# A state-space and expert block on one core: the state's output by 64-row matmuls in pairs

## The reference

```python
xz = layernorm(x) @ w_in;  xp, z = split(xz, 2)            # 512 channels each
xc = silu(causal_conv4(xp) + conv_b)
def step(h, xt):
    h = h * 0.9 + 0.1 * (xt @ w_B)                         # w_B: 512 x 16
    return (h, h @ w_C)                                    # w_C: 16 x 512
_, ys = scan(step, 0, xc)
x = x + (ys * silu(z)) @ w_out
...
h = gelu(x_norm @ W1[e] + b1[e]);  x = x + sum over 2 experts of (h @ W2[e] + b2[e]) / 2
```

## Time and profile before

| | us |
|---|---|
| median of 3 runs | 508.88 (508.84 to 509.13) |
| the profiled execution, its own time | 509.31 |
| its span, first to last instruction | 507.5 |
| PE busy | 503.0 (99%) |
| DVE busy | 452.3 (89%) |
| ACT busy | 400.7 (79%) |
| POOL busy | 348.2 (69%) |
| granted TensorE clock | 1.000 of full |

### The profile page before, as it was taken

One profiled execution on the slowest core, in us unless ns is written; L12 is line 12 of the kernel. 1 busy time (PEld: TensorE's weight loads), 2 busy tenths in 40 slices (PEclk: granted clock), 3 DMA queues, 4 the chain that ended last, 5 costly groups with the idle time before them and its releaser, 6 DMA issues.

```text
span 507.5 us, 9839 instructions
## 1 busy us (share of the span) xinstructions
PE 503.0 (99%) x3026; PEld 447.6 (88%) x3026; DVE 452.3 (89%) x896; ACT 400.7 (79%) x692; POOL 348.2 (69%) x390
## 2 busy tenths in 40 slices
PE   8999999999999999999999999999999999999997
PEld 8889799898898989989899998989989899998997
DVE  6999899999998899989999899998999989996773
ACT  4986958878869788697887969779797887969454
POOL 4959597659693796928969197772977649673391
PEclk9999999999999999999999999999999999999999
DMA  8940005344251432606235170432604333130102
GB/s 266 292 174 12 32 0 173 119 131 162 74 182 37 165 124 83 206 17 193 79 124 165 42 223 24 165 124 86 203 40 143 106 125 125 51 115 0 43 3 83
DMA packets 53379, 57.28 MB, mean 113 GB/s; under 512 B 8682, under 2 KB 49642, under 8 KB 53226
## 3 DMA queue, kind: packets, MB, share of 16 engines
q1 hardware_dynamic: 51498, 56.67, 34.1%
q10 hardware_dynamic: 1856, 0.31, 0.3%
HBM read 35.46 MB, written 21.50 MB: 112 GB/s over the span
## 4 chain that ended last, share of the span: by engine, by line
PE 97%; DVE 1%; DMA 1%; issue 0%; DVEq 0%
PE blk L1291 16%; PE blk L1292 16%; PE blk L1296 16%; PE tok L1410 12%; PE tok L1408 12%; PE tok L1409 12%; PE turn L1449 3%; PE turn L1452 3%; PE blk L1471 3%; PE turn L1239 1%; PE tok L1291 1%; PE tok L1296 1%; PE tok L1292 1%; DMA x_mid<-in_L_attn_x 1%; DVE stats_t L914 0%; DVE normed L931 0%
## 5 line engine op out<-in xcount | busy, mean ns | idle before, releaser
L989 DVE SCALAR_TENSOR_TENSOR conv<-blk,tap_w,conv 128x512 f32<-128x512 f32 x192 | 130.1, 740 | 8.2 <-ACT conv L680 7.6
L485 POOL TENSOR_TENSOR y_lo<-gate,y_hi 128x512 fp32r<-128x512 f32 x57 | 72.2, 1299 | 36.6 <-ACT y_hi L608 36.5
L1291 PE MATMUL blk<-xn_hi,w_in_hi 128*128 128x512 f32 x228 | 89.5, 393 | 0.0
L1292 PE MATMUL blk<-xn_hi,w_in_lo 128*128 128x512 f32 x228 | 89.1, 391 | 0.0
L450 POOL TENSOR_TENSOR xc_lo<-conv,xc_hi 128x512 fp32r<-128x512 f32 x60 | 72.7, 1229 | 8.3 <-ACT xc_hi L608 8.1
L1408 PE MATMUL tok<-w_out_hi,y_hi 128*128 128x256 f32 x256 | 72.1, 282 | 0.0
L1410 PE MATMUL tok<-w_out_hi,y_lo 128*128 128x256 f32 x256 | 71.9, 281 | 0.0
L1409 PE MATMUL tok<-w_out_lo,y_hi 128*128 128x256 f32 x256 | 71.9, 281 | 0.0
L1296 PE MATMUL blk<-xn_lo,w_in_hi 128*128 128x512 f32 x228 | 70.3, 389 | 0.0
L1408 PE MATMUL tok<-w_hi,hid_hi 128*128 128x256 f32 x248 | 69.9, 282 | 0.0
L1410 PE MATMUL tok<-w_hi,hid_lo 128*128 128x256 f32 x248 | 69.7, 281 | 0.0
(11 more groups left out here) (189 smaller groups left out, 1321.7 us busy)
## 6 DMA issues: line engine op xcount, KB each, us to landing
spill<-normed SPq DMA_DIRECT2D x25, 512.0 KB, 2.8
normed<-spill SPq DMA_DIRECT2D x100, 128.0 KB, 2.8
out<-x_mid SPq DMA_DIRECT2D x30, 256.0 KB, 2.7
x_mid<-in_L_attn_x SPq DMA_DIRECT2D x29, 256.0 KB, 2.7
x_in<-in_L_attn_x SPq DMA_DIRECT2D x14, 512.0 KB, 4.3
w_all<-in_L_ffn_W SPq DMA_DIRECT2D x2, 2048.0 KB, 11.8
b_all<-in_L_ffn_b SPq DMA_DIRECT2D x1, 1024.0 KB, 13.1
gate<-in_L_attn_w_in SPq DMA_DIRECT2D x2, 256.0 KB, 4.5
```

The costliest lines, as they stand in the source:

```text
L485: nc.gpsimd.tensor_tensor(y_lo[:, j, :], gate_of(o, j), y_hi[:, j, :].bitcast(F32), ALU.subtract).then_inc(y_lo_set, 1)
L989: nc.vector.scalar_tensor_tensor(cols, blk[j][:], tap_w[:, j, t:t + 1], cols, ALU.mult, ALU.add).then_inc(tap_added, 1)
L1291: mm(dst, whi(k), his(k), start=(k == 0), stop=False)
L1292: mm(dst, wlo(k), his(k), start=False, stop=False)
```

## The change

- **TensorE.** `state_out` multiplies over 64 rows in place of 128. Blocks 0 and 2 use rows 0 to 63 of `c_mix` and `state_mix`, blocks 1 and 3 rows 64 to 127. Still four matmuls of 512 columns, into the same banks, in the same order. In the steps (not in the opening) the wait for a free bank is taken for two blocks at a time, ahead of the first of them, so the second has no wait.
- **Layout.** Each half of 64 rows is the same: four groups of 16, where `b_mix` holds w_B rounded in groups 0, 1, 2 and the rest of w_B in group 3. `state_mix` becomes: rounded state in groups 0, 2, 3 and the rest of the state in group 1. `c_mix`: rounded w_C in groups 0, 1, 3 and the rest in group 2. The products of two rests are left out.
- **Masks.** Four columns of one number per row are made once by VectorE from the identity matrix at the start (`row_masks`): `low_rows` is 1 in the group that holds a rest and 0 elsewhere, `sign_rows` is -1 there and 1 elsewhere.
- **ScalarE** now rounds state times `sign_rows` (a scale read per row, in place of a constant); **VectorE** does state * `low_rows` + `state_mix` over 128 rows in one scalar_tensor_tensor, in place of a subtraction over 64 rows; **GpSimd**, for chunk 1, does it in two instructions, one that multiplies the state by the mask and, after a wait on it, an addition.
- **Constants in the opening.** `b_mix`: three ScalarE instructions of 128 numbers per row in place of four of 64, two GpSimd subtractions in place of four. `c_mix`: a GpSimd multiplication and an addition over 128 rows in place of two subtractions over 32 rows.

```diff
+        def mix_cols(h, group):
+            return slice(h * HALF + group * NST, h * HALF + (group + 1) * NST)
...
             def state_lo(a, q):
                 pool.wait_ge(norm2_ready, TT - EARLY)
                 pool.wait_ge(h_hi, a + 1)
-                nc.gpsimd.tensor_tensor(state_mix[P // 2:P, :], state[P // 2:P, q, :],
-                                        state_mix[P // 2:P, :].bitcast(F32), ALU.subtract).then_inc(h_lo, 1)
+                nc.gpsimd.tensor_scalar(state[:, q, :], state[:, q, :], low_rows[STATE][:], None, ALU.mult).then_inc(h_masked, 1)
+                pool.wait_ge(h_masked, 1)
+                nc.gpsimd.tensor_tensor(state_mix[:], state[:, q, :], state_mix[:].bitcast(F32), ALU.add).then_inc(h_lo, 1)
...
             def state_hi(a, q):
                 act.wait_ge(scanned, a + 1)
-                hi(state_mix[:], state[:, q, :]).then_inc(h_hi, 1)
+                hi(state_mix[:], state[:, q, :], sign_rows[STATE][:]).then_inc(h_hi, 1)
...
             def state_lo(a, q):
                 dve.wait_ge(h_hi, a + 1)
-                lo(state_mix[P // 2:P, :], state[P // 2:P, q, :], state_mix[P // 2:P, :]).then_inc(h_lo, 1)
+                nc.vector.scalar_tensor_tensor(state_mix[:], state[:, q, :], low_rows[STATE][:], state_mix[:].bitcast(F32), ALU.mult,
+                                               ALU.add).then_inc(h_lo, 1)
...
+            def row_masks():
+                dve.wait_ge(consts_set, 3)
+                groups = ident[:].rearrange("p (h g i) -> p g h i", h=2, i=NST)
+                for i, group in enumerate(LOW_GROUP):
+                    nc.vector.tensor_reduce(low_rows[i][:], groups[:, group], axis=mybir.AxisListType.XY,
+                                            op=ALU.add).then_inc(rows_set, 1)
+                for i in range(2):
+                    dve.wait_ge(rows_set, 1 + i)
+                    nc.vector.tensor_scalar(sign_rows[i][:], low_rows[i][:], -2.0, 1.0, ALU.mult, ALU.add).then_inc(rows_set, 1)
+
             def opening():
+                row_masks()
...
             def state_out(a, s, js=range(JD)):
                 pe.wait_ge(h_lo, a + 1)
...
-                    mm(c_bank(a, j)[:], c_mix[:, j * P:(j + 1) * P], state_mix[:], start=True,
+                together = 2 if has_ffn(s) else 1
+                for i, j in enumerate(js):
+                    if i % together == 0:
+                        c_free(a, s, js[i + together - 1])
+                    rows = slice(j % 2 * HALF, (j % 2 + 1) * HALF)
+                    mm(c_bank(a, j)[:], c_mix[rows, j * P:(j + 1) * P], state_mix[rows, :], start=True,
                        stop=True).then_inc(c_ready, 1)
```

More of the change, by code:

```diff
@@ L35, in build_block @@
     HALO = TAPS - 1
-    REP = P // (2 * NST)
-    assert PER == 2 and TT == 4 and KD == 2 and JD == 4 and JF == 4 and NST == 16 and E == 8
+    HALF = P // 2
+    STATE, WEIGHT = 0, 1
+    LOW_GROUP, REST_GROUP = (1, 2), 3
+    assert PER == 2 and TT == 4 and KD == 2 and JD == 4 and JF == 4 and HALF == 4 * NST and E == 8
     x_t = x.rearrange("b s d -> (b s) d").rearrange("(c n p) d -> c p n d", p=P, n=TT)
@@ L66, in build_block @@
         unused = sb("unused", [1, 1])
+        low_rows, sign_rows = [sb(f"low_rows{i}", [P, 1]) for i in range(2)], [sb(f"sign_rows{i}", [P, 1]) for i in range(2)]
         first_tok = sb("first_tok", [P, KD])
@@ L117, in build_block @@
         consts_set = sem("consts_set")
+        rows_set = sem("rows_set")
         w_hi_set = sem("w_hi_set")
@@ L148, in build_block @@
         u_ready, scanned = sem("u_ready"), sem("scanned")
-        h_hi, h_lo = sem("h_hi"), sem("h_lo")
+        h_hi, h_masked, h_lo = sem("h_hi"), sem("h_masked"), sem("h_lo")
         c_ready = sem("c_ready")
@@ L512, in opening @@
                 norm1(1)
-                pool.wait_ge(w_hi_set, 5 + REP)
-                for r in range(REP):
-                    nc.gpsimd.tensor_tensor(b_mix[:, :, (2 * r + 1) * NST:(2 * r + 2) * NST], wb_raw[:],
-                                            b_mix[:, :, 2 * r * NST:(2 * r + 1) * NST].bitcast(F32),
-                                            ALU.subtract).then_inc(mix_lo_set, 1)
-                for i, r in enumerate((P // 4, 3 * P // 4)):
-                    rows = slice(r, r + P // 4)
-                    pool.wait_ge(mix_lo_set, REP + i)
-                    nc.gpsimd.tensor_tensor(c_mix[rows, :], state[rows, 0, :], c_mix[rows, :].bitcast(F32),
-                                            ALU.subtract).then_inc(mix_lo_set, 1)
-                pool.wait_ge(mix_lo_set, REP + 2)
+                pool.wait_ge(w_hi_set, 5 + REST_GROUP)
+                for h in range(2):
+                    nc.gpsimd.tensor_tensor(b_mix[:, :, mix_cols(h, REST_GROUP)], wb_raw[:],
+                                            b_mix[:, :, mix_cols(h, 0)].bitcast(F32), ALU.subtract).then_inc(mix_lo_set, 1)
+                pool.wait_ge(rows_set, 4)
+                nc.gpsimd.tensor_scalar(state[:, 0, :], state[:, 0, :], low_rows[WEIGHT][:], None, ALU.mult).then_inc(mix_lo_set, 1)
+                pool.wait_ge(mix_lo_set, 3)
+                nc.gpsimd.tensor_tensor(c_mix[:], state[:, 0, :], c_mix[:].bitcast(F32), ALU.add).then_inc(mix_lo_set, 1)
+                pool.wait_ge(mix_lo_set, 4)
                 split_conv(0, (0, 1))
@@ L624, in mix_hi @@
                 hi(state[:, 0, :], raw_c, GAIN).then_inc(w_hi_set, 1)
-                for r in range(REP):
-                    hi(b_mix[:, :, 2 * r * NST:(2 * r + 1) * NST], wb_raw[:]).then_inc(w_hi_set, 1)
-                act.wait_ge(w_hi_set, 4 + REP)
-                hi(c_mix[:], state[:, 0, :]).then_inc(w_hi_set, 1)
+                for group in range(REST_GROUP):
+                    both = b_mix[:].rearrange("p j (h c) -> p j h c", h=2)[:, :, :, mix_cols(0, group)]
+                    hi(both, wb_raw[:].rearrange("p j (o s) -> p j o s", o=1).broadcast_to([P, JD, 2, NST])).then_inc(w_hi_set, 1)
+                act.wait_ge(w_hi_set, 4 + REST_GROUP)
+                act.wait_ge(rows_set, 4)
+                hi(c_mix[:], state[:, 0, :], sign_rows[WEIGHT][:]).then_inc(w_hi_set, 1)
             def turn1_hi(c):
@@ L1453, in state_in, with c_free @@
                 ins.then_inc(u_ready, 1)
+            def c_free(a, s, j):
+                if has_ffn(s):
+                    pe.wait_ge(gelu_set, (s - 2) * JF + j + 1)
+                elif a == 0:
+                    pe.wait_ge(gate_set, JD + j + 1)
+                elif j == 0:
+                    pe.wait_ge(route_step, 1)
+                elif j == 1:
+                    pe.wait_ge(tap_added, last_tap(2, 2))
+                elif j == 2:
+                    pe.wait_ge(gate_set, 3 * JD - 1)
+                else:
+                    pe.wait_ge(tap_added, last_tap(2, 3))
             def state_out(a, s, js=range(JD)):
                 pe.wait_ge(h_lo, a + 1)
[L1457 to L1471 removed]
+                together = 2 if has_ffn(s) else 1
[4 more added lines that the diff above has]
+                    mm(c_bank(a, j)[:], c_mix[rows, j * P:(j + 1) * P], state_mix[rows, :], start=True,
                        stop=True).then_inc(c_ready, 1)
```

19 lines of the change are left out of this document (3 added, 16 removed).

## The result

The changed kernel takes 511.9 us (median of 4 runs, 511.66 to 513.09) where the kernel before, run beside it, takes 509.0: a ratio of 1.0061, with a 95% interval of 1.0044 to 1.0079. The prediction said 506.4 and a range of 505.0 to 510.0. It is slower, not faster, and outside the range. The profiled execution took 511.66 with a span of 509.8 (before 509.31 and 507.5), so the traces stand 2.3 us apart.

What follows compares the result with a forecast made beforehand. TensorE, busy 99%, was taken as the bound, if VectorE (89%) keeps up. Boundary gains of 3.28 us less 0.80 lost in the opening gave -2.48: 506.8 profiled, 506.4 in medians; range 505.0 to 510.0.

Steps and rivals of the forecast that it cites:

- I take no price for the change of form: TensorE at state_out: switching matmul form costs nothing, so each state_out takes 0.56 us for 0.93, a gain of 0.37.
- a change of form costs as much as an exposed load on either side: Rival at state_out: 0.10 us lost on either side, gain 0.17 per state_out, 508.0 us in all; chance 0.12.
- I let the second of a pair start 0.10 late: TensorE at state_out: the second matmul's exposed weight load delays it 0.10 us; starts at 0, 0.10, 0.23, 0.33.
- the rival's pairs: Rival at state_out: both loads go ahead, a pair costs 0.23 us and state_out 0.46; 505.8 us in all; chance 0.12.
- the array must empty: Rival at state_out: emptying at each form change adds 0.52 us, 1.08 against 0.93; 511.8 us in all; chance 0.12.
- Its threshold: Emptying decides once both changes cost over 0.30 us together: gain per place below 0.07, twelve places no longer pay the opening.
- I count 0.13: Boundaries without score after chunks 6, 8, 10, 12: room 0.32 less 0.06 and 0.14, counted 0.13 us gained each, 0.52 together.
- The chain: State's chain on ScalarE and VectorE: rounding +0.09 us, state_lo +0.05, so 0.14 longer, between 0.05 and 0.25; covered at state_out.
- VectorE late at the taps: One of the signs listed as showing the prediction wrong: VectorE late at the taps; no size given.
- GpSimd in the opening: Chunk 1's state_lo on GpSimd: multiplication 1.00 us, +1.27 in all, less 0.48 room; TensorE loses 0.80, between 0.4 and 0.9.
- pairs gain ahead of this place: Opening, chunks 0 and 1: any gain from pairs is swallowed by TensorE's wait for GpSimd's w1_lo; no size given.
- The masks: Opening: four VectorE instructions, about 1 us from 1.5 on, hidden ahead of first statistics, which wait for x until 3.96.

Runs made afterwards that it cites:

- kernel with the parts alone: Changed kernel with state_out's four matmuls over all 128 rows again, masks, layout and the other engines' new forms kept: 510.48 us, ratio 1.0029 to the kernel before.
- with one half: Changed kernel with all four state_out matmuls on rows 0 to 63, one after another: 516.86 us, ratio 1.0152 to the kernel before.
- with pairs three times over: Changed kernel with each state_out's four 64-row matmuls run three times over, in the loop and after it: 522.85 us, ratio 1.0270 to the kernel before.
- with two visits: Changed kernel with ys(0) earlier and the opening's two edits, state_out's pairs split by six 128-row matmuls from chunk 3 on: 514.11 us, against 508.87 unsplit.

## Why the prediction was wrong

- **TensorE, the step that failed first: "I take no price for the change of form".** It costs 0.39 us per visit, so that a `state_out` gains 0.07 where 0.37 was counted. I had read from the router's matmuls an exposed load of 0.10 and nothing lost beyond it, and took that as proof that changes are free. But those keep all 128 rows; only the columns differ. The count of rows is what costs. In size this is the rival "a change of form costs as much as an exposed load on either side", with two such loads on either side instead of one.
- **The pairing was underestimated.** I let the second of a pair start 0.10 late; it starts 0.003 late, so a pair costs 0.23, not 0.33. The Trainium skill, "TensorE: Matmul & The Clock Gate", Part 3, has about 4 ns, and the trace agrees. With the rival's pairs (0.46 for four) and my free changes the sum would have been still further off.
- **The rival "the array must empty" named 511.8, and 511.9 was measured, but not by its sum.** It had `state_out` 0.15 slower; it is 0.07 faster. The page behind it ("TensorEngine Tiling (Array Packing)", Key Properties, also of the Trainium skill) says that a change of mode drains TensorE. A price per change there is, 0.19 to 0.20 each, where 0.26 was worked out. Whether it is emptying or two loads that can't go ahead these traces don't tell: the load's record starts with its matmul in either case. That 511.8 fell so near 511.9 is luck: its loss was to come from TensorE in every step, the measured one came from five boundaries and the opening. Its threshold was near the truth: the net gain measured per place, 0.07, is the value below which it said that the places no longer pay for the opening.
- **The boundaries without score: "I count 0.13" each.** Five of them lose 0.34 each. That the load of `xp` would wait for ys there was forecast. But the room of 0.32 was read as fixed, and only the shift of TensorE and the chain were taken off it. The chain was forecast well: ScalarE 0.72 (0.72 predicted), `state_lo` 0.75 undisturbed (0.74), and beside GpSimd 0.93, where the kernel before took 1.02. What was not asked is what TensorE's other timing does to VectorE against GpSimd: 0.45 us of VectorE's time, at every second boundary. The list of what would be wrong had "VectorE late at the taps"; it is late behind them.
- **GpSimd in the opening: 0.80 predicted, 2.0 lost.** Two terms were too small: the multiplication, 1.57 for 1.00, beyond my upper bound of 1.10, which came from doubling a 256-column instruction of the same kind; and what "pairs gain ahead of this place", which was to be swallowed by the wait and was a loss of 0.66 (0.26 at chunk 0's first three matmuls, 0.40 at the lone one) that went into GpSimd's start. The kernel with the parts alone, without that loss, starts GpSimd's multiplication at 53.25 and is 1.46 behind at chunk 2. The path itself (mask, addition, xc_lo, w_lo, TensorE) was the predicted one; the load of the earlier trace rows came at 61.63, where 60.4 was named.
- **The masks** were hidden, as said (the four instructions lie between 1.55 and 2.01 us, half of the 1 us that was taken, and the first statistics start at 3.98); ScalarE's and VectorE's extra load cost nothing in the loop, as the kernel with the parts alone shows.

## What to carry to other kernels

Before packing small matmuls into parts of the array, count visits, not matmuls: here each change between 128 and 64 rows and back cost 0.39 us and each pair saved 0.23, so two pairs barely pay, one pair loses, and six pairs in one visit would, by an estimate from these two figures, gain 6 x 0.23 - 0.39 = 1.0. When an engine at its bound is made faster, read the neighbours' slack as something that moves with it: take the second engine's long gapless run, look which third engine's instructions stand beside it and which of the two starts first by a few tenths, and keep an order at hand that puts the awaited tile first.

## Not expected of the hardware

- A change of the row count costs TensorE two late starts of about 0.10 us each, at entry and at exit alike (0.39 to 0.40 per visit in the changed kernel, with one half, with pairs three times over and with two visits), while inside the form starts are 0.23 apart, as over 128 rows.
- A VectorE instruction of four columns took 0.16 or 1.07 us, depending on whether a GpSimd instruction of 1.1 us had started just before it, and a subtraction of 512 columns 0.69 or 1.67, depending on which of the two engines started first; a shift of 0.27 us between the engines turned this order round, and through it TensorE lost 0.34 us per two steps.
- GpSimd's multiplication by a scalar per row took 1.57 us for 128 x 512, with SBUF operands, at both places where it stands (17.77 and 53.70), where its additions of two tiles take 1.29 and 1.30.
- Between kernels, what lies around the span differs: 1.8 us in most, 2.0 in the four in which the changed kernel's opening was edited (as 510.65 with a span of 508.6, or 508.35 with 506.3). A part of what the opening gained is lost there. What causes it was not tried.
